# A scan with a routed feed-forward on one core: the feed-forward's plan dealt by slots, two projections split, b3 added on GpSimd

## The reference, cut to what matters

```python
def xattn(hidden, z, ...):                    # hidden = ctx (4, 1024, 512), z = layernorm(x)
    xs = einsum('ed,bld->bel', in_proj_w, hidden)            # in_proj
    u = silu(causal_conv4(xs, conv_w) + conv_b)
    dt_lo, Bm, Cm = split(einsum('ke,bel->bkl', x_proj_w, u))  # x_proj: 32 + 16 + 16 rows
    delta = softplus(dt_proj_w @ dt_lo + dt_proj_b)
    # for each time step: state = state * exp(delta * A) + (delta * u) * B;  y = sum_n state * C
    ...
    return swapaxes((y + D * u) * silu(z), 1, 2)

def ffn(x, ...):                              # x = layernorm(x1)
    logits = x.reshape(b, -1) @ switch_w.T + switch_b        # one decision per batch, 8 experts
    gate, top = top_k(softmax(logits), 2)
    o = sum_k gate_k * (gelu(x_head @ w1[top_k].T + b1) @ w2[top_k].T + b2)   # 16 heads of 64
    return (x + o) @ w3.T + b3

x1 = x + xattn(ctx, layernorm(x), ...)
out = x1 + ffn(layernorm(x1), ...)
```

## Time and profile before

| | us |
|---|---|
| median of 3 runs | 2473.86 |
| lowest, highest | 2465.63, 2474.52 |
| the profiled execution's own time | 2471.16 |
| its span, first to last instruction | 2469.3 |
| DVE, PE, ACT, POOL busy in it | 2133.6, 2013.5, 1602.4, 1445.2 |

### The profile page before, as it was taken

The page is one execution under the profiler, slowest core; times in us unless marked ns, Lnnn a source line. Parts: engine busy times, 40 slices in busy tenths (PEclk is TensorE's granted clock), DMA queues, the critical chain, the costliest instruction groups (busy, mean ns, idle before and its releaser), DMA issues.

```text
span 2469.3 us, 32717 instructions
## 1 busy us (share of the span) xinstructions
PE 2013.5 (82%) x10776; PEld 1203.1 (49%) x10776; DVE 2133.6 (86%) x2712; ACT 1602.4 (65%) x2357; POOL 1445.2 (59%) x993
## 2 busy tenths in 40 slices
PE   6798888985757997996675897898685798797899
PEld 2677676653433553454453454454453455344344
DVE  5899789979999899998999899998999899999322
ACT  2677787656669868655667878855576857954500
POOL 0588677767756566566675566665775666665000
PEclk9899889997878998997888999899787899999899
DMA  5311434555612754566542464466460174578412
GB/s 174 128 37 52 150 99 148 188 162 169 246 37 103 261 166 133 161 204 203 188 155 74 140 232 152 147 224 199 154 239 26 60 253 145 164 251 283 168 56 72
DMA packets 200329, 383.01 MB, mean 155 GB/s; under 512 B 31553, under 2 KB 97089, under 8 KB 200162
## 3 DMA queue, kind: packets, MB, share of 16 engines
q1 hardware_dynamic: 196992, 380.47, 46.1%
q10 hardware_dynamic: 3170, 0.47, 0.1%
HBM read 346.80 MB, written 34.08 MB: 154 GB/s over the span
## 4 chain that ended last, share of the span: by engine, by line
PE 44%; DVE 19%; issue 17%; ACT 14%; POOL 3%; DMA 1%; DVEq 0%; SPq 0%; ACTq 0%; POOLq 0%
PE dense L1135 13%; PE dense L962 9%; DVE h L1525 9%; PE dense L900 5%; ACT dA L1246 4%; PE dense L948 3%; DVE dense L1501 3%; POOL h L865 3%; DVE u L1357 2%; PE dense L912 2%; PE dense L1112 2%; ACT L1213 2%; PE dense L921 2%; PE dense L1065 2%; PE dense L969 2%
## 5 line engine op out<-in xcount | busy, mean ns | idle before, releaser
L865 POOL TENSOR_TENSOR h<-h,Cb 128x1024 f32<-128x1024 f32 x512 | 1208.4, 2361 | 431.8 <-DVE h L1525 408.2
L1246 ACT ACTIVATE dA<-delta,Av 128x512 f32<-128x512 f32 x1024 | 703.1, 717 | 384.6 <-DVE h L1525 381.3
L962 PE MATMUL dense<-ident,h 128*128 128x128 f32 x4096 | 605.4, 299 | 165.0 <-POOL h L865 163.5
L962 PEld LDWEIGHTS dense<-ident,h 128*128 128x128 f32 x4096 | 521.1, 155 | 315.6 <-POOL h L865 225.8
L1525 DVE TENSOR_TENSOR_SCAN h<-dA,state,dense 128x512 f32<-128x512 f32 x512 | 627.4, 1263 | 31.0 <-issue 14.4
L1525 DVE TENSOR_TENSOR_SCAN h<-dA,dense 128x512 f32<-128x512 f32 x512 | 596.7, 1203 | 22.0 <-PE dense L962 8.5
L1501 DVE TENSOR_TENSOR dense<-dense,Bb 128x512 f32<-128x512 f32 x864 | 550.5, 682 | 1.6
L1135 PE MATMUL dense<-w3h,xT 128*128 128x512 f32 x832 | 386.0, 598 | 0.0
L859 POOL COPY state<-h 128x2 f32<-128x2 f32 x256 | 47.6, 186 | 336.6 <-DVE h L1525 335.1
L948 PE MATMUL dense<-Bb,duT 128*128 128x128 f32 x1280 | 179.9, 289 | 41.1 <-DVE h L1525 31.7
L1135 PEld LDWEIGHTS dense<-w3h,xT 128*128 128x128 f32 x832 | 147.9, 192 | 130.1 <-issue 130.1
(11 more groups left out here) (168 smaller groups left out, 2084.1 us busy)
## 6 DMA issues: line engine op xcount, KB each, us to landing
sww<-in_sw SPq DMA_DIRECT2D x167, 512.0 KB, 4.2
Cb<-bc_scratch SPq DMA_DIRECT2D x64, 512.0 KB, 6.1
Bb<-bc_scratch SPq DMA_DIRECT2D x54, 512.0 KB, 4.6
w3h<-in_sw SPq DMA_DIRECT2D x52, 512.0 KB, 8.2
w3h<-in_w3T SPq DMA_DIRECT2D x52, 512.0 KB, 5.2
row<-x_scratch SPq DMA_DIRECT2D x40, 512.0 KB, 4.5
xz<-in_x SPq DMA_DIRECT2D x64, 256.0 KB, 4.7
xt<-in_x SPq DMA_DIRECT2D x64, 256.0 KB, 3.9
```

Of the source, the lines that this page charges most:

```text
L865: e.tensor_tensor(h[:, s:s + 2, :], h[:, s:s + 2, :], Cb[:, 2 * q:2 * q + 2, :], ALU.mult).then_inc(prod_done, 1)
L962: mm = e.matmul(yT[:, k, :], h[:, 2 * ((PAIRS * g + q) % RH) + i, k * P:(k + 1) * P], ident[:], is_transpose=True, start=False, stop=(q == ...
L1246: e.activation(dA[:, i % RA, :], delta[:, st % 2, :], ACT.Exp, scale=Av[:, j * N + n:j * N + n + 1]).then_inc(dA_done, 1)
```

## The change

It touches the plan, and the engines' programs where the plan's items changed.

1. `hidden` of half 0 moves from slots 39, 41, ... 53 to 39, 41, 45, 48, 50, 53, 56, 58; in batches 1 and 2 (`SPILL`) that of half 1 from 83, 85, ... 97 to 91, 93, 96, 98, 101, 104, 106, 109. In batch 3 it begins at 85. Where a gelu stands in slot 6 of a step, the table load between silu and gelu is left out.
2. The 32 parts of a half are dealt by `spread`, which has a number for the room of each slot on PE (nearly none in slot 2 of a step, none in the two slots of x_proj, 17 less where half an in_proj stands). In batches 1 and 2 the second half's parts lie in 112 to 140, that is up to slot 12 of the next batch. So items now carry the batch that they belong to (`fb`).
3. `in_proj` is issued in two halves, `in_proj` and `in_proj_end`, in two slots, as x_proj was already. `ln1_stats` is two items, `ln1_sum` and `ln1_square`, in two slots. `ln1_rstd` and `ln1_shift` stand in slots 70 and 72 instead of 124 and 126 (`r1`, `nm1` have two buffers for it).
4. `b3` is loaded once into `duT`'s room at slot 33 of batch 1, and POOL adds it to `res` (`b3_add`) two slots after the tile's first part, for all 64 tiles. PE's transposes and the tail's additions on DVE are gone. DVE's `tile_out` waits for that addition instead of the load of `res`.
5. The tail's ring of switch weights takes a piece of `h` instead of `duT`; statistics and logits of batches 1 and 2 stand 1 to 7 slots later, those of batch 3 three.

```diff
+SPILL = (1, 2)
+HIDDEN = [39, 41, 45, 48, 50, 53, 56, 58]
...
     def add(self, b, t, *what):
+        if b < NB and t >= STEPS * SLOTS:
+            b, t = b + 1, t - STEPS * SLOTS
         self.slots[b][t].append(what)
...
             if st % J == J - 1 and 0 < g < ALL - AHEAD + 1:
                 self.add(b, t, "in_proj", st - 1)
+                self.add(b, t + 1, "in_proj_end", st - 1)
...
             if g + AHEAD < ALL and st % J != J - 2:
                 self.add(b, t + 6, "in_proj", st)
+                self.add(b, t + 7, "in_proj_end", st)
         if b + 1 < NB:
             for k in range(J):
-                rows.append((b, 54 + 3 * k // 2, "ln1", k))
-                self.add(b, 57 + 3 * k // 2, "ln1_stats", k)
-            self.add(b, 124, "ln1_rstd")
-            self.add(b, 126, "ln1_shift")
+                t = 54 + 3 * k // 2
+                rows.append((b, t, "ln1", k))
+                self.add(b, t + 3, "ln1_sum", k)
+                self.add(b, t + 4, "ln1_square", k)
+            self.add(b, t + 6, "ln1_rstd")
+            self.add(b, t + 8, "ln1_shift")
...
+        spill = b in SPILL
+        hidden = [HIDDEN, [91, 93, 96, 98, 101, 104, 106, 109] if spill else list(range(85, 101, 2))]
+        tiles = [self.spread(b, 60, 88, ()) if spill else self.spread(b, 60, 82, ()),
+                 self.spread(b, 112, 141, range(112, 120)) if spill else self.spread(b, 102, 128, range(102, 116))]
...
-            at = [tiles + m * span // (2 * TB * W3C) for m in range(2 * TB * W3C)]
+            at = tiles[u]
             for dh in range(NQ):
                 for k in range(TB):
                     m = W3C * (TB * dh + k)
-                    self.add(b, at[m], "res_load", u, dh, k)
+                    self.add(b, at[m], "res_load", b, u, dh, k)
+                    self.add(b, at[m] + 2, "b3_add", b, u, dh, k)
                     for c in range(W3C):
-                        self.add(b, at[m + c], "tile", u, dh, k, c)
-                    self.add(b, at[m + W3C - 1] + 2 if at[m + W3C - 1] < 126 else 127, "tile_out", u, dh, k)
+                        self.add(b, at[m + c], "tile", b, u, dh, k, c)
+                    self.add(b, at[m + W3C - 1] + 2, "tile_out", b, u, dh, k)
...
+    def spread(self, b, first, end, logits):
+        def room(t):
+            g, q = STEPS * b + t // SLOTS, t % SLOTS
+            st = g % J
+            left = [29, 40, 1, 29, 23, 29, 29, 29][q]
+            if st == J - 1:
+                left = [29, 40, 11, 19, 23, 29, 29, 29][q]
+            if st == J - 2 and q >= 6 and g + J < ALL:
+                left = 0
+            elif st != J - 2 and q >= 6 and g + AHEAD < ALL or st == J - 1 and q < 2 and g < ALL - AHEAD + 1:
+                left -= 17
+            return left - (6 if t in logits else 0)
+        n = 2 * TB * W3C
+        whole = sum(max(room(t), 1) for t in range(first, end))
+        at, done = [], 0
+        for t in range(first, end):
+            done += max(room(t), 1)
+            while len(at) < n and (2 * len(at) + 1) * whole <= 2 * n * done:
+                at.append(t)
+        return at
...
+                    elif what == "b3_add":
+                        fb, uu, dh, k = a
+                        n = part_index(fb, uu, dh, k, 0) // W3C
+                        e.wait_ge(b3_loaded, 1 + 16)
+                        e.wait_ge(res_loaded[n % 2], 1 + 16 * (n // 2 + 1))
+                        e.tensor_tensor(res[:, n % 2], res[:, n % 2], b3row[:, dh, :], ALU.add).then_inc(b3_added, 1)
...
-                        exp_ln_table()
+                        if b == NB or not any(what == "gelu" for what, *a in PLAN.slots[b][t]):
+                            exp_ln_table()
...
-                        e.wait_ge(res_loaded[n % 2], 1 + 16 * (n // 2 + 1))
-                        if b == NB:
-                            e.wait_ge(b3_loaded, 1 + 16)
-                            e.tensor_tensor(res[:, n % 2], res[:, n % 2], b3row[:, dh, :], ALU.add).then_inc(b3_added, 1)
-                            e.wait_ge(b3_added, 1 + n - 2 * NQ * TB * (NB - 1) + 1)
+                        e.wait_ge(b3_added, 1 + n + 1)
```

153 lines of the change are left out of this document (80 added, 73 removed).

## The result

The changed kernel takes **2496.0 us** (median of 6 runs, 2483.2 to 2500.4), the kernel before in runs beside it 2470.9 (2465.6 to 2474.5). The ratio is 1.010, 95% interval 1.0083 to 1.0118: 1% slower, where I had forecast 28 us less, had given 77% to a gain of over 12.4 us, and had a range of 2430 to 2467. Five of the six runs lie at 2494.5 to 2500.4 and one at 2483.2. The profiled execution is one of the five. The profiled executions span 2497.8 us and 2469.3.

What follows compares the result with a forecast made beforehand. DVE was taken as the bound, with only its standstill to win: -11.9 - 9.0 - 4.6 - 3.7 + 0.6 + 0.3 = -28.3 us from 2473.9 gives 2445.6, said as 2446; 8-in-10 range 2430 to 2467.

Steps and rivals of the forecast that it cites:

- Steps 14 and 15: Second x_proj, batches 1 and 2: standstill falls to 5.1 us from 13.0 (batch 2: 11.7).
- Waits for b3: DVE waits 2.4 us for POOL's addition at one tile in batches 1 and 2, two in batch 3; 9.7 in all.
- Step 7: Two gelus among the first statistics lengthen ACT's chain to `delta`; step stands still 7.0 us, 3.3 more; batch 3 1.4.
- Steps 5 and 6: Three gelus a step instead of four: standstill 6.1 us against 8.9, in batch 3 against 10.9.
- rival (a): PE's clock falls where it idles; first x_proj 7 us longer in three batches, +21, 2467 us; chance 0.12.
- Steps 8 to 13: Batches 1 and 2: step 8 stands still 3.9 us against 2.3; in steps 9 to 13 1.7 remain of 7.9 and 7.1.
- Batch 0: Split statistics take 1.3 us from a tap, `ln1_shift` saves 2.4 of its wait: -3.7, bounds -8 and +1.
- Steps 0 to 2 of batches 2 and 3: Parts run over into the next batch, switch weights load late: 0.8 us, twice, bounds 0 and 5 each.
- Batch 3: Standstill 17.0 us against 21.6, with 1.4 in step 7 and 7.0 in steps 8 to 15.
- Tail: Last addition on DVE goes, 0.69 us; last parts in slot 127 put the last sum back by 1.0: together +0.3.
- Rival (c): POOL becomes the bound for output tiles through late `res` loads or blocking with DVE: slower, 2507 us; chance 0.07.

Runs made afterwards that it cites:

- e_out4: `e_unsplit_even` with the addition of a tile to its residual at least four slots behind the residual's load: 2463.3 us.
- e_old_only: The changed kernel with only the first half's units put back to 39, 41, 43 ... 53, as before the change: 2474.8 us.
- e_unsplit_h1: The changed kernel with in_proj in one slot and only the second half's units of batches 1 and 2 moved to even slots: 2473.7 us.
- e_unsplit_even: The changed kernel with in_proj back in one slot and no gelu in an odd slot of a step: 2467.2 us.
- e_before_split: The kernel before the change, with only the last four of in_proj's eight blocks put one slot later: 2477.6 us.
- e_gelu_even: The changed kernel with expert units moved by one slot wherever a gelu stood in an odd slot of a step: 2488.4 us.
- e_comb_split: The changed kernel with first-half units at the old pace, second-half in even slots, tile additions four slots behind residual loads, run-over to slot 137: 2451.5 us.
- e_ue_outlate: `e_unsplit_even` with an edit meant to put tile additions three slots behind residual loads, which moved no instruction: 2467.9 us.

## Why the prediction was wrong

The forecast was 56.8 us off (-28.3 against +28.5 between the two profiled executions). By its own terms, in us of VectorE's standstill:

- **Steps 14 and 15: right.** 5.4 in batches 1 and 2, predicted 5.1. The gap at 1.120 is 5.25 (4.6), that at 1.123 is gone:

```profile
1121.67 2.45 DVE L1572 TENSOR_TENSOR_SCAN h<-dA,state,dense 128x512 f32<-128x512 f32 x2 [5.25 <-issue]
```

- **Waits for b3: right.** 2.6 us at 1.67, 2.67, 3.72 and 3.83, predicted 2.4 at just these places. But without them (`e_out4`) the kernel was 4 us faster, not 10.

```profile
880.72 0.69 DVE L1536 TENSOR_TENSOR res<-dense,res 128x512 f32<-128x512 f32 x1 [2.58 <-POOL res L934]
```

- **Step 7: the number right, its price misjudged.** 6.4 and 6.7, predicted 7.0, with 4.92 ahead of `delta` at 1.59 (predicted 6.8 there) and 1.44 at the tap. My own sign for it, 6 to 7 us ahead of `delta`, was missed. I had booked 3.3 us as the price of a pace that was to save 2.8 us in steps 5 and 6 (4.8 in batch 3) and more in 8 to 13, and never put this pace against the old one with the rest of the change. With that one row put back (`e_old_only`) batches 1 to 3 are 13.6 us shorter.
- **Steps 5 and 6: the first term that failed, in batches 1 and 2 with the wrong sign.** Predicted 6.1 in place of 8.9 (10.9 in batch 3); measured 12.6 and 10.3 in batches 1 and 2, 10.6 in batch 3. I had lowered ScalarE's *load* (31.3 and 27.8 us of work in place of 34.8 and 34.0; 29.7 and 28.9 predicted) and taken the standstill to follow. It followed the order: at 1.51 a gelu stands ahead of softplus (1.91 us at `delta`), at 1.54 an expert_out waits behind the slow first half of x_proj (2.93 us at `xT`, 0.67 before). By `e_unsplit_h1` the odd slots are 1.2 us of each step 6 (1.8 in batch 3). And rival (a) came here after all, by its own sign, a half of x_proj over 5 us: 1.8, 1.3 and 1.5 us more in the three batches, in one half of the two, where I had priced it at 7. Against it I had set that `hidden` and the sums directly ahead keep TensorE at work; but the `hidden` of slot 53 is done early, and behind it come 4.25 us without work.
- **Steps 8 to 13: the largest miss.** 3.9 us in step 8 and 1.7 in the rest predicted; step 8 is 3.5 and 3.2, but steps 9 to 13 are 8.7 and 11.2, of which steps 12 and 13 are 8.3 and 9.7. With even slots and the whole in_proj (`e_unsplit_even`) these two are 1.3 and 1.5. For these steps I had written "gelus fall with shared loads" and looked at no slot.
- **Batch 0: sign wrong.** -3.7 predicted, bounds -8 and +1; measured +12.3 in the profiled execution, 11.9 of it in steps 2, 4 and 6. LN1's part came as predicted (step 9 2.1 us less, step 8 1.3 less idle), and -4.2 is what batch 0 shows with in_proj whole. The split I had costed at nothing, since the eight blocks are the same work and PE had room. I never asked what stands behind the moved half. In this profile the mechanism was rival (a)'s, the clock, in a place where I had not looked for it. With the same code of batch 0 and no fall of the clock (`e_old_only`) it is +0.6, within the bounds but still 4.3 over the forecast. That the falls come only in some executions was in no bound. What makes them come stays open.
- **Steps 0 to 2 of batches 2 and 3:** 0.8 more than before predicted, with bounds of 0 and 5; measured 3.2 and 2.6, mostly ahead of slot 16 and at its tap. TensorE's wait for switch weights in w3's room, shown above, is the path that the text gave for the bound.
- **Batch 3:** step 7 1.4 predicted, 2.9 measured; steps 8 to 15 7.0, and 8.3.
- **Tail:** +0.3 predicted, +6.0 in the profiles. One program showed 198.9 and 202.9, and the kernels with the new tail's plan 198.9 to 203.1, with the old one 194.6 and 197.0. By the medians (199.8 of fifteen, 195.8 of two) about 4 us are there, of which 1.4 is the longer wait for the first late row (3.41 us against 1.97). The gap ahead of the last sum of the switch's logits grew from 19.6 to 24.4 us; in it one of four reloads of rows landed after 7.2 us, where the median of the four is 6.0, and TensorE ran below its clock behind a wait of 4.0 us. What of this is the plan's and what chance stays open; ending the tiles earlier did not help. The start-up took 79.9 us against 78.9, within what the other kernels show (78.5 to 79.9).

Rival (c) did not come: GpSimd has 1525 us of work, and VectorE's times are untouched by its 64 further additions. The 154.9 us of idle time ahead of them in the rows below all lie in the tail; in the batches none of the 48 additions waited for its load.

```profile
L1572 DVE TENSOR_TENSOR_SCAN h<-dA,state,dense 128x512 f32<-128x512 f32 x512 | 628.0, 1265 | 31.8 <-PE dense L1013 12.6
...
L934 POOL TENSOR_TENSOR res<-res,duT 128x512 f32<-128x512 f32 x64 | 81.4, 1273 | 154.9 <-DMA res<-x_scratch 154.9
...
L1536 DVE TENSOR_TENSOR res<-dense,res 128x512 f32<-128x512 f32 x64 | 43.9, 686 | 110.2 <-PE dense L1182 93.4
```

A tile's addition takes 686 ns, where it took 683. The Trainium skill's rule on the shared port ("SBUF — State Buffer", Who interferes with whom) leaves out VectorE instructions with at most one input in SBUF, as this one is, and the trace agrees: nothing is seen of it here.

Two readings in the working were off without weight in the sum: step 12 of batch 2 stood still 0.8 us longer than that of batch 1 and not the same, and 13 us and ten parts of 1.81 are 31 us, not 30 (measured 31.2 in step 0 of batch 2).

The range failed because its terms were taken as independent and small errors; it held no case in which an edit costed at nothing had a price.

## What to carry to other kernels

Where in-order queues feed each other, the load of an engine over a step says little about who waits; walk each moved instruction through its queue and name what stands behind it up to the next thing the bound engine needs (here softplus behind a gelu, transposes behind half an in_proj). Splitting work evenly between slots is not neutral even if an engine has room. One profile of a kernel with two groups of runs shows one of them, so look at all runs before a difference between two profiles is put down to the edit. And single edits can each look small (1.7 and 7.6 us) while together they give 28.8, so undo suspected parts in pairs as well.

## What the runs showed of the hardware

TensorE's granted clock can fall behind waits of under 2 us: in the changed kernel it was 0.66 from 137 to 152 us, behind waits of 1.42 and 1.78 us. Waits of the same lengths at the same places left it at 1.00 in `e_old_only` and `e_before_split`, so their length alone doesn't forecast it. The same instructions have more than one steady rhythm: steps 2 to 5 of batch 0 took 30.9, 27.1, 30.9, 27.1 us in the changed kernel, 27.1, 30.9, 27.1, 30.9 in `e_gelu_even`, and 27.3 each, at a clock of 1.00 throughout, in `e_old_only`, though none of these edits touches batch 0:

```profile
133.20:160.30 27.10, 23.75 (x161) 19.62 (x160) 24.90 (x28) 19.59 (x31) 22.07 (x19) 0.94 0.14 39
160.30:191.20 30.90, 27.70 (x176) 23.41 (x175) 25.16 (x28) 20.45 (x32) 23.32 (x19) 0.83 0.12 36
```

```profile
130.30:157.60 27.30, 23.19 (x168) 19.12 (x167) 24.82 (x28) 20.03 (x31) 22.59 (x18) 1.00 0.13 40
157.60:184.90 27.30, 23.17 (x168) 19.11 (x167) 24.84 (x29) 20.03 (x31) 22.60 (x18) 1.00 0.13 40
```

The first pair is `e_gelu_even`, the second `e_old_only`. It would explain the two groups of runs, 9 to 16 us apart, that `e_before_split`, `e_old_only`, `e_comb_split` and by one run the changed kernel show, all of them with the split. That the groups are these two rhythms is seen in one profile of each kernel, not in every run. Without the split one such step was seen alone: step 3 of batch 0 took 30.1 us at a clock of 0.83 in `e_ue_outlate`, and 27.2 in `e_unsplit_even`, the same program.
